# Four layers of a graph network on one Trainium2 core: SyncE brings fourteen gather tiles a layer instead of seven

## What is computed

```
h = relu(layernorm(x));  x += mean over edges and self of (h @ W)[src] + b
h = relu(layernorm(x));  lap = segment_sum(h[src] * w, dst)
                         x += unit(leaky((h + lap) @ W1 + b1 + (h * lap) @ W2 + b2))
h = relu(layernorm(x));  m = (h @ Wn + bn)[src] * ssp(ssp(e @ We1 + be1) @ We2 + be2)
                         x += ssp(segment_sum(m, dst) @ Wf1 + bf1) @ Wf2 + bf2
h = relu(layernorm(x));  GAT with 4 heads: softmax over each node's edges and itself,
                         mean over heads, layernorm, relu, + h;  added to x
```

## Time and profile before

| | |
|---|---|
| median of 3 runs | 4121.83 us (4121.44 to 4122.98) |
| span of the profiled execution | 4118.2 us, the only time there is of it |
| instructions | 65293 |
| POOL busy | 2981.3 us, 72% |
| DVE busy | 2593.0 us, 63% |
| PE busy (matmul) | 2408.9 us, 58% |
| ACT busy | 1816.6 us, 44% |
| indirect gathers on POOL (L756) | 3100, mean 945 ns |
| row fetches on SP | 3584 |

### The profile page before, as it was taken

One profiled execution on the slowest core, in us unless ns is written; L12 is line 12 of the kernel. 1 busy time (PEld: TensorE's weight loads), 2 busy tenths in 40 slices (PEclk: granted clock), 3 DMA queues, 4 the chain that ended last, 5 costly groups with the idle time before them and its releaser, 6 DMA issues. The chain is left out here.

```text
span 4118.2 us, 65293 instructions
## 1 busy us (share of the span) xinstructions
PE 2408.9 (58%) x13340; PEld 2021.0 (49%) x13340; DVE 2593.0 (63%) x7266; ACT 1816.6 (44%) x4202; POOL 2981.3 (72%) x3172
## 2 busy tenths in 40 slices
PE   3666666655566666656544444444566666666667
PEld 2555555554454555546434334443554555454556
DVE  5444444443566666667644444444669999999997
ACT  3444444422243444432211111111457887788886
POOL 4777777776777777777677777777757777777763
PEclk8787777777677787877765666656779999999899
DMA  7444444432344443432333333333466222222221
GB/s 148 125 116 126 116 126 116 126 83 69 94 116 125 116 124 115 126 106 67 100 110 105 110 105 105 110 105 109 115 117 124 58 57 58 57 57 57 57 53 32
DMA packets 242878, 405.96 MB, mean 99 GB/s; under 512 B 68322, under 2 KB 141691, under 8 KB 242492
## 3 DMA queue, kind: packets, MB, share of 16 engines
q0 software_dynamic: 99456, 206.27, 20.8%
q10 hardware_dynamic: 69920, 120.96, 10.4%
q1 hardware_dynamic: 73116, 74.56, 6.2%
HBM read 331.90 MB, written 67.79 MB: 97 GB/s over the span
## 5 line engine op out<-in xcount | busy, mean ns | idle before, releaser
L756 POOL DMA_INDIRECT t_work<-d_T,t_tabG x3100 | 2928.1, 945 | 1038.5 <-issue 848.1
L1657 PE MATMUL ps<-t_work,t_acc 128*128 x2592 | 463.0, 340 | 439.7 <-POOLq L723 396.5
L1657 PEld LDWEIGHTS ps<-t_work,t_acc 128*128 128x128 f32 x2592 | 414.9, 245 | 516.9 <-issue 516.6
L1730 DVE TENSOR_TENSOR t_acc<-t_acc,ps 128x128 f32 (+1 forms) x732 | 210.3, 287 | 513.6 <-PE ps L594 209.5
L1832 ACT COPY ps<-t_acc 128x512 f32 x244 | 140.6, 588 | 779.1 <-POOLq L723 777.1
L1719 DVE TENSOR_TENSOR t_hT<-t_work,ps 128x512 f32<-128x512 f32 x244 | 167.2, 685 | 503.0 <-ACT ps L1832 502.9
L1657 PE MATMUL ps<-t_hT,t_acc 128*128 128x128 f32 x1296 | 264.0, 388 | 272.2 <-DVE t_acc L1730 263.4
L1657 PEld LDWEIGHTS ps<-t_hT,t_acc 128*128 128x128 f32 x1296 | 249.1, 295 | 288.9 <-DVE t_hT L1719 285.0
L1657 PE MATMUL ps<-t_work 128*128 x1312 | 239.9, 347 | 249.7 <-POOLq L723 220.2
L627 ACT ACTIVATE t_acc<-ps,t_bcol 128x1024 f32<-128x1024 f32 x98 | 109.1, 1113 | 612.4 <-DVE ps L640 590.5
L2145 PE MATMUL ps<-t_work,t_hT 128*128 x1960 | 316.8, 310 | 100.2 <-DVE t_acc L2155 81.9
(11 more groups left out here) (205 smaller groups left out, 4478.6 us busy)
## 6 DMA issues: line engine op xcount, KB each, us to landing
d_edge_net<-t_acc ACTq DMA_DIRECT2D x98, 512.0 KB
t_acc<-d_edge_net SPq DMA_DIRECT2D x98, 512.0 KB, 4.2
t_work<-d_T,t_tabG POOLq DMA_INDIRECT x3100
t_acc<-in_edge_attrT ACTq DMA_DIRECT2D x96, 512.0 KB, 4.2
t_acc<-d_T SPq DMA_DIRECT2D x1792, 0.5 KB
t_acc<-d_T SPq DMA_DIRECT2D x896, 0.5 KB
t_work<-d_T SPq DMA_DIRECT2D x896, 0.5 KB
t_acc<-d_T ACTq DMA_DIRECT2D x12, 790.1 KB, 17.0
```

The costliest lines, as they stand in the source:

```text
L756: pool.indirect_dma_start(out=work[:, at:at + width], out_offset=None, in_=table, in_offset=bass.IndirectOffsetOnAxis(ap=idx[:, g * QUAD + ...
L1657: last = pe.matmul(sums(layer, s, width), masks[s % MASKS][:, k, :], rows_k, start=(k == 0), stop=(k == QUAD - 1))
L1730: dve.tensor_tensor(out=o, in0=o, in1=sums(layer, s, width), op=ALU.add).then_inc(e_acc[layer], 1)
```

## The change

SyncE brings 14 tiles a layer, ten rows per group, so the groups in SIDE_AT are 23, 36, ..., 190. It keeps 32 sources in registers, loaded at once from an address that is now rounded up to a multiple of four words, and uses them up over several groups. The tables of loop numbers become 16-bit, made through 32-bit scratch and then copied. SP reads eight closings at a time, POOL 32. ACT's control numbers and the slots, windows and needs of layer 3 are read for two steps (needs: eight) at once. SIDE_READS grows from 14 to 28.

```diff
@@ -8,6 +8,7 @@
 U8 = mybir.dt.uint8
+U16 = mybir.dt.uint16
 ALU = mybir.AluOpType
@@ -32,7 +33,7 @@
 AHEAD = 5
-SIDE, SIDE_PER, SIDE_READ = 7, 5, 64
+SIDE, SIDE_PER, SIDE_READ, SIDE_REGS = 14, 10, 64, 32
 SIDE_BEGIN = [-(-(P * j) // SIDE_PER) for j in range(SIDE + 1)]
@@ -42,7 +43,7 @@
 SIDE_READS = SIDE * P // SIDE_READ
-assert P % SIDE_READ == 0
+assert P % SIDE_READ == 0 and SIDE_READ % SIDE_REGS == 0 and SIDE_READS % 2 == 0
 assert SIDE_AT[-1] < GROUPS
@@ -162,12 +163,12 @@
         idx, dstf, wgt = tabG[:, 0:TILES].bitcast(I32), tabG[:, TILES:2 * TILES], tabG[:, 2 * TILES:3 * TILES]
-        ctl = sb("ctl", [1, 4 * (STEPS + LEAD)], I32)
-        closing, closing2 = sb("closing", [1, GROUPS], I32), sb("closing2", [1, GROUPS], I32)
+        ctl = sb("ctl", [1, 4 * (STEPS + LEAD)], U16)
+        closing, closing2 = sb("closing", [1, GROUPS], U16), sb("closing2", [1, GROUPS], U16)
         relB = sb("relB", [P, TABB])
-        winB, slotB = sb("winB", [1, TABB], I32), sb("slotB", [1, TABB], I32)
-        needB, closingB = sb("needB", [1, TABB // QUAD], I32), sb("closingB", [1, GROUPS], I32)
+        winB, slotB = sb("winB", [1, TABB], U16), sb("slotB", [1, TABB], U16)
+        needB, closingB = sb("needB", [1, TABB // QUAD], U16), sb("closingB", [1, GROUPS], U16)
         wts = sb("wts", [P, 8, D])
@@ -423,17 +424,18 @@
         need(dve, ld_g.mark)
-        V.did(dve.tensor_scalar(closing[:], lastrow, 7, None, ALU.arith_shift_right))
-        m_shift = V.did(dve.tensor_scalar(closingB[:], lastrow, WB.bit_length() - 1, None, ALU.arith_shift_right))
+        group_w, quad_w, pair_w = (take(GROUPS)[0:1, :].bitcast(I32) for _ in range(3))
+        V.did(dve.tensor_scalar(group_w, lastrow, 7, None, ALU.arith_shift_right))
+        V.did(dve.tensor_scalar(quad_w, lastrow, WB.bit_length() - 1, None, ALU.arith_shift_right))
         m = V.did(dve.tensor_scalar(shifted_g, lastg, 7, None, ALU.arith_shift_right))
         need(dve, m, ld_c.mark)
-        V.did(dve.tensor_copy(closed_w, closing[:]))
+        V.did(dve.tensor_copy(closed_w, group_w))
         closed_q = take(GROUPS)[0:1, :]
...
         need(dve, m_q)
-        m_q = V.did(dve.tensor_tensor(out=closingB[:], in0=closingB[:], in1=closed_q, op=ALU.add))
+        m_q = V.did(dve.tensor_tensor(out=quad_w, in0=quad_w, in1=closed_q, op=ALU.add))
         need(dve, m_q)
-        V.did(dve.tensor_scalar(closingB[:], closingB[:], 2, None, ALU.arith_shift_right))
+        m_q = V.did(dve.tensor_scalar(quad_w, quad_w, 2, None, ALU.arith_shift_right))
         m = V.did(dve.tensor_tensor(out=end_g, in0=shifted_g, in1=cst[:, x0:x0 + 2], op=ALU.add))
@@ -453,11 +455,13 @@
         V.did(dve.tensor_scalar(ctl3[:, LEAD:STEPS + LEAD, 2], win_s[:, 0:STEPS], float(ACC3), None, ALU.mult))
-        m_end = V.did(dve.tensor_tensor(out=closing[:], in0=closed_w, in1=steps[0:1, 1:GROUPS + 1], op=ALU.add))
-        need(dve, m, m_end)
-        m = V.did(dve.tensor_scalar(closing2[:], closing[:], 1, None, ALU.add))
+        V.did(dve.tensor_tensor(out=closing[:], in0=closed_w, in1=steps[0:1, 1:GROUPS + 1], op=ALU.add))
+        m_end = V.did(dve.tensor_tensor(out=pair_w, in0=closed_w, in1=steps[0:1, 2:GROUPS + 2], op=ALU.add))
+        need(dve, m, m_end, m_q)
+        m = V.did(dve.tensor_scalar(pair_w, pair_w, 1, None, ALU.arith_shift_right))
+        V.did(dve.tensor_copy(closingB[:], quad_w))
         need(dve, m)
-        V.did(dve.tensor_scalar(closing2[:], closing2[:], 1, None, ALU.arith_shift_right))
+        V.did(dve.tensor_copy(closing2[:], pair_w))
         V.did(dve.tensor_scalar(ctl3[:, 0:STEPS + 1, 3], slot_s, float(QUAD * ACC3), None, ALU.mult))
@@ -678,12 +682,6 @@
-        def control(engine, s):
-
-            edge, win, off, slot = numbers(engine, ctl[0:1, 4 * s:4 * s + 4], 4, 0, NT * ACC3)
-            return (within(edge, QUAD, TILES), within(win, 0, NT), within(off, 0, (NT - 1) * ACC3),
-                    within(slot, 0, (RING - 1) * PITCH))
-
         RAW_GROUP = RING // 2
@@ -723,7 +721,7 @@
         SAID_BEHIND = 2
-        ENDS = 14
+        ENDS = 32
@@ -777,11 +775,11 @@
-            row = acc[0:1, NT * ACC3:XC] if layer < 3 else work[0:1, (RING * QUAD + 2) * ROW3:]
-            return row[:, c % 2 * SIDE_READ:(c % 2 + 1) * SIDE_READ].bitcast(I32)
-
-        assert MLP + 11 * GRP + 2 * ACC3 <= BB * ACC3 and NT * ACC3 + 2 * SIDE_READ <= XC
-        assert (RING * QUAD + 2) * ROW3 + 2 * SIDE_READ <= work.shape[1] and SIDE_READS % 2 == 0
+            held, lo = (acc, -(-NT * ACC3 // 4) * 4) if layer < 3 else (work, -(-(RING * QUAD + 2) * ROW3 // 4) * 4)
+            assert lo + 2 * SIDE_READ <= (XC if layer < 3 else work.shape[1])
+            return held[0:1, lo + c % 2 * SIDE_READ:lo + (c % 2 + 1) * SIDE_READ].bitcast(I32)
+
+        assert MLP + 11 * GRP + 2 * ACC3 <= BB * ACC3
@@ -789,22 +787,22 @@
+        row_from = {}
+
         def fetch_rows(layer, table, n):
...
             table_b = table.rearrange("n w -> (n w)").unsqueeze(0).bitcast(U8)
-            for c in range(SIDE_READS):
-                lo, hi = [min(max(SIDE_PER * m - SIDE_READ * c, 0), SIDE_READ) for m in (n, n + 1)]
-                if lo == hi:
-                    continue
-                if lo == 0:
+            for r in range(SIDE_PER * n, min(SIDE_PER * (n + 1), SIDE * P)):
+                c, at = divmod(r, SIDE_READ)
+                if at == 0:
                     sp.wait_ge(s_src[c % 2], 16 * (SIDE_READS // 2 * layer + c // 2 + 1))
-                found = numbers(ENG.SP, side_sources(layer, c)[:, lo:hi], hi - lo, 0, (N - 1) * row)
-                for r, at in zip(range(c * SIDE_READ + lo, c * SIDE_READ + hi), found):
-                    j, p = divmod(r, P)
-                    sp.dma_start(side_rows(layer, j)[p:p + 1, :].bitcast(U8)[:, 0:row], table_b[:, bass.ds(at, row)])\
-                        .then_inc(s_row[layer][j % 4], 16)
-                if hi == SIDE_READ and c + 2 < SIDE_READS:
+                if at % SIDE_REGS == 0:
+                    row_from[layer] = numbers(ENG.SP, side_sources(layer, c)[:, at:at + SIDE_REGS], SIDE_REGS, 0, (N - 1) * row)
+                j, p = divmod(r, P)
+                sp.dma_start(side_rows(layer, j)[p:p + 1, :].bitcast(U8)[:, 0:row],
+                             table_b[:, bass.ds(row_from[layer][at % SIDE_REGS], row)]).then_inc(s_row[layer][j % 4], 16)
+                if at == SIDE_READ - 1 and c + 2 < SIDE_READS:
                     read_sources(layer, c + 2)
@@ -833,15 +831,15 @@
             for n in range(GROUPS):
-                if n % 4 == 0:
-                    ends = numbers(ENG.SP, closed_at[0:1, n:n + 4], 4, 1, top_at)
+                if n % 8 == 0:
+                    ends = numbers(ENG.SP, closed_at[0:1, n:min(n + 8, GROUPS)], min(8, GROUPS - n), 1, top_at)
                 if layer == 3 and n + AHEAD < GROUPS:
...
                     fetch_rows(layer, table, n)
-                sp.wait_ge(used, ends[n % 4])
+                sp.wait_ge(used, ends[n % 8])
                 sp.sem_inc(e_free[layer] if layer < 3 else s_paced, 1)
@@ -1823,9 +1821,13 @@
+            found = []
+
             def bring(s):
-                edge, _, _, slot = control(ENG.Activation, s)
+                if s % 2 == 0:
+                    found[:] = control_pair(ENG.Activation, s // 2)
+                edge, _, _, slot = found[s % 2]
                 act.wait_ge(e_rdy[2], edge)
@@ -2028,10 +2030,14 @@
+        def two_quads(n):
+
+            return slice(QUAD * n, QUAD * (n + 2))
+
         def slots_of(engine, n):
-            return [within(v, 0, (RING * QUAD - 1) * ROW3)
-                    for v in numbers(engine, slotB[0:1, steps_of(n)], QUAD, 0, (RING * QUAD - 1) * ROW3)]
+            v = numbers(engine, slotB[0:1, two_quads(n)], 2 * QUAD, 0, (RING * QUAD - 1) * ROW3)
+            return v[:QUAD], v[QUAD:]
@@ -2136,9 +2142,13 @@
+        rows_at = {}
+
         def sum_step(n):
-            slots = slots_of(ENG.PE, n)
+            if n % 2 == 0:
+                rows_at[n], rows_at[n + 1] = slots_of(ENG.PE, n)
+            slots = rows_at[n]
             pe.wait_ge(s_cp, n + 1)
@@ -2159,18 +2169,19 @@
-            if add in range(QUADSB):
-                sums_at[add] = numbers(ENG.DVE, winB[0:1, steps_of(add)], QUAD, 0, (BB - 1) * ACC3)
+            if add in range(0, QUADSB, 2):
+                v = numbers(ENG.DVE, winB[0:1, two_quads(add)], 2 * QUAD, 0, (BB - 1) * ACC3)
+                sums_at[add], sums_at[add + 1] = v[:QUAD], v[QUAD:]
...
-            if head in range(QUADSB):
-                rows_of[head] = slots_of(ENG.DVE, head)
+            if head in range(0, QUADSB, 2):
+                rows_of[head], rows_of[head + 1] = slots_of(ENG.DVE, head)
...
-            if head in range(QUADSB) and head % 4 == 0:
-                needs[head // 4] = numbers(ENG.DVE, needB[0:1, head:head + 4], 4, 1, TILES)
+            if head in range(0, QUADSB, 8):
```

(3 more changed lines are left out.)

## The result

The changed kernel takes 4418.28 us (median of 4 runs, 4417.86 to 4423.27) where the kernel before takes 4121.64 on the same chip: a ratio of 1.0722, interval [1.0707, 1.0737]. The forecast was 4086.8, the range 4080 to 4105. The four rows that answer to the earlier trace rows are the gathers' line of the changed kernel by layer, with first and last start.

A forecast was written before the change was run, and what follows sets the result against it. POOL's unbroken gathers were taken to bound all four layers; 28 fewer give -35.1 us and every other term 0, so the span goes from 4118.2 to 4083.1 and the median from 4121.8 to 4086.8, range 4080 to 4105.

The forecast's parts named there:

- Step 6: 16-bit tables and paired reads: eight 16-bit numbers load as one aligned piece at 0.34 us, nobody on the path gains.
- Rival B: DVE's slot and window reads in layer 3: 16-bit numbers come one by one, +223 us, about 4318; chance 0.07.
- Step 1: POOL's gathers: 7 fewer in every layer, 28 x 1.2535 = 35.1 us off.
- Steps 2 to 5: SyncE's rows, load of 32 sources (2.3 us), late announcements in layer 3, and placing: all hidden, cost 0.
- Step 7: Table making on DVE ahead of the loop: about two more instructions, under 1 us, counted as 0.
- Rival A: Layer 3 gives nothing, as late announcements meet DVE at 95%: 4095.5 us; chance 0.13.
- Rival D: Fewer gathers change nothing, since something other than POOL bounds; chance 0.03.

The follow-up runs named there:

- f3_slots32: The changed kernel without SyncE's tiles, slots and windows of layer 3 at 32 bits, the other tables 16-bit: 4183.37 us, 1.0157 of the kernel before.
- f2_alone32: The changed kernel without SyncE's tiles (POOL gathers all 782 a layer) and with all tables 32-bit: 4157.42 us against 4118.35 for the kernel before.
- e1_fifth: The changed kernel with all tables 32-bit, SyncE's fourteen tiles and paired reads kept: 4091.21 us against 4121.33 for the kernel before.
- e1_again: The changed kernel with all tables 32-bit, run at a time when SyncE's instructions were late: 5454.1 us against 5108.2 for the kernel before.

## Why the prediction was wrong, by its steps

**Step 6 failed.** "I take the first, because all the aligned 32-bit rows behave so": no row had a 16-bit load, and the near rows were near in alignment, not in width. The bound from above was right (8 x 0.226 = 1.81; measured 1.83), and so was the place. The same step put the paired reads at nothing ("nobody on the path gains"): with 16-bit numbers they carry about 146 of the 314 us. Rival B, which had the one-by-one price, got a chance of 0.07 and should have had something like an even one, since nothing in the trace spoke of width. The Trainium skill (Runtime: NRT & Kernel Launch, "Instruction fetch mechanics") gives about 200 ns a register even in bulk, of loads from HBM. For these loads from SBUF that holds for 16-bit numbers (228) and for unaligned 32-bit ones (6.73 / 32 = 210), and not for aligned 32-bit ones (2.13 / 32 = 67).

**Rival B** gave 4318. Its uncovered 1.1 us a step is measured as 179.1 / 155 = 1.16. It left out the needs (30.0 / 155 = 0.19 a step) and took 3.74 for the rest where 5.16 - 1.35 = 3.81 stand: 5.16 in place of 4.85, 76 us over the steps. The other 16-bit tables, control numbers and closings, go with 10 us before layer 2 (the first of POOL's eight gathers at L700 waits 10.1 for SP's free), 4 before layer 3 and 5 in layer 1; f3_slots32 shows the same turns 12 and 4 us longer than f2_alone32. Which of the two it is was not tried apart.

**Step 1 held.** In the changed kernel layers 0 and 2 are 8.1 and 7.2 us shorter (8.8 forecast); from the other side, 28 more gathers than before cost f2_alone32 39.1 us; e1_fifth gains 30.1 of 35.1, and 3.4 of the missing 5 are layer 3's. What lies outside the gathers is 4118.2 - 3881.1 = 237 us and not 234; the forecast doesn't use it.

**Steps 2 to 5 held.** The load of 32 took 2.13 (2.3), SP's work in layer 2 is 4.65 us a group (4.60), late announcements cost 1.4 us in 800. **Step 7** can't be told from 0: the first gather starts at 41.1 for 40.9.

**Rival A** is partly so: layer 3 gives 5.4 of 8.8, not because announcements are late but because DVE is full. The argument against it had DVE need 3.74 us a step, its busy time while it still waited for others; in e1_fifth its work and its own waits take 782.6 + 14.3 = 796.9 us for 206 steps, 3.87 a step, and the 3.90 on hand leave next to nothing. **Rival D** is out.

The right forecast would have been two-sided: 4087 if width doesn't matter, 4318 or more if it does, with no row to choose by. The range of 4080 to 4105 left the second out.

## What to carry to other kernels

A register load was priced here by how it is cut, not by its bytes: halving the tables' width tripled the price of eight numbers (0.60 to 1.83 us). Keep loop tables 32-bit, start each load at a multiple of four words, and put it behind an operation at least as long. Where each number has its price, several short loads, each behind an operation, lose less than one long load behind one. When a change alters the type or width of an operand and no row shows its price, give both times, one for each price; rows that are like it in another respect can't choose. An engine whose loads are hidden (0.34 behind 0.68 before, 0.60 behind 0.68 in e1_fifth) shows no idle time for them and says nothing of what a dearer load would cost: once it outlasts the cover, all the rest is paid at every step.

## What the runs showed of the hardware

Medians of loads into registers from SBUF, in us. 32-bit numbers: four 0.34 and eight 0.60 on DVE, 32 aligned 2.04 on POOL and 2.13 on SP, 32 unaligned 6.73 on SP. 16-bit numbers: four 0.945 and eight 1.83 on DVE, 14 3.14 and 32 7.11 on POOL. On DVE, PE and POOL the median of one load moved by 1% at most from run to run. On SP it depends on what SP does beside: eight aligned 32-bit closings of layer 3 take 0.52 in f2_alone32, where SP fetches no rows, and 0.69 in e1_fifth.

SyncE itself can be slow where nothing else is. In a trace of e1_again SP's move before a row's fetch takes up to 1.4 us, and 28 fetches take 14.52 us; in e1_fifth no move is over 40 ns, and 44 take 18.01. One row of each view, first e1_again, then e1_fifth.

```profile
L803 SPq MOVE t_acc<-d_T x5376: 1/29/1398, 86.9 to 3832.2; - x200
...
606.11 14.52 SPq L803 DMA_DIRECT2D t_acc<-d_T  x28
```
```profile
L803 SPq MOVE t_acc<-d_T x5376: 29/29/40, 66.6 to 2903.8; - x200
...
599.89 18.01 SPq L803 DMA_DIRECT2D t_acc<-d_T  x44
```

In the stretches that are late, one instruction starts some 0.7 us after another: in the trace of e1_again 2031 of SyncE's start 0.6 to 0.8 us behind the one before, in that of e1_fifth 108. The same count is 822 and 785 on DVE, 115 and 120 on ACT, and POOL's "issue" before gathers is 859.6 and 849.8 us: these engines are not slower. It is no property of the kernel (the kernel before takes 5098 to 5188 us at such times) nor of a chip for good: chip 4 gave 5188 us for the kernel before at one time and 4121 at another. Its cause stays open. It does say that a plan with SyncE at 95% of the pace, as in layer 2 of e1_fifth, has no room for it: at such times fourteen tiles a layer with 32-bit tables (e1) cost 6.5 to 7.0% over seven, where they otherwise gain 0.7%.
